# The loads between two layers, issued before the barrier instead of behind it

## The chip, the cores and the metric

The kernel runs on one core of one Trainium2 chip. The metric is the time of one execution on the device, in microseconds (us), as the median of several runs. The times of single instructions come from one profiled execution of the same kernel. TensorE is called PE, VectorE DVE, ScalarE ACT, GpSimd POOL and SyncE SP.

## The reference

Two layers follow each other over 3327 nodes with 256 features. Each is a graph attention over an adjacency matrix and then a mixture of experts, both added to the running x:

```python
x = x + _L0_gnn_ref(_layernorm(x), adj, L0_gnn_W, L0_gnn_r)
x = x + _L0_ffn_ref(_layernorm(x)[None], ...)[0]      # 8 experts, the best 2 of each node
x = x + _L1_gnn_ref(_layernorm(x), adj, ...)          # 4 heads, bias and a projection of the inputs
x = x + _L1_ffn_ref(_layernorm(x)[None], ...)[0]      # 8 experts, the best 2 of each node
```

What matters here is the seam between the second and the third line. The output of the first layer's experts is whole only when every expert's contribution has been added to every node; then a layer norm of it feeds the second layer's projections.

## The kernel before

The nodes are padded to 26 tiles of 128 rows. `X` in SBUF holds 26 x 256 float32 words per partition; `arena` holds everything else.

**The experts of layer 0** (`X0`) run over 59 tiles of slots. For each tile PE computes the hidden layer (L2308) and the output (L2347), DVE adds the bias and scales (L2427, L2430), and POOL scatters the 128 rows with an accumulating indirect DMA (L2296) into one of two totals in DRAM: `xd` for even tiles, `xe` for odd ones. Each scatter counts on one of two semaphores, `added[0]` and `added[1]`. While the experts run, `X` serves as room for their intermediates, so it can be loaded again only when the last scatters have read it. At the end of `tiles_gpsimd` POOL waits for both semaphores to be full.

**The program is cut into blocks.** In a block each engine has its own instruction list. At the end of a block every engine executes a drain and meets the others at a barrier (in the profile these instructions carry the line of the next block's `with`, L2502). Between the second block (layer 0) and the third (layer 1) there follow a clearing of the first layer's semaphores by POOL (L2558) and one more barrier (L2559).

**The third block begins with `A1.back_load`** (L484). It brings the two totals back: `xd` into `X` by four DMAs issued by SP, and `xe` into `A1.other` (a part of `arena`), its first piece by ACT and the other three by POOL. The pieces are cut at the pairs `PIECES = (0, 2, 5, 9, 13)` of tiles, so they hold 4, 6, 8 and 8 tiles of 128 KB. Each piece has a semaphore for each total. Behind its four loads SP runs `give_ones` (L2479): it adds one to each semaphore that has to start at one, those by which ACT, PE and DVE take turns over buffers among them. POOL adds up the two biases (L590), for which DVE waits before it begins with the pieces.

**The pieces** are then worked on as they come. DVE adds the two totals of a pair of tiles (L497, in `add_stats`), takes the statistics of both tiles (L501), and after the last pair of a piece computes mean and deviation (`norm_of`, L2452 to L2465 and L506; the square root, L2471, is ACT's). ACT normalizes a tile (L563), PE transposes it (L703), ACT copies it out (L548), and PE computes the projection (L713) and the attention's products (L716). DVE's `keep` (L514) adds the projection into `X` and frees its PSUM bank for PE. The order on each engine is written out by hand:

```python
for j in range(pieces[1]):          # pieces_vector, DVE
    add_stats(j)
norm_of(0)
for c in range(1, 4):
    for j in range(pieces[c], pieces[c + 1]):
        add_stats(j)
        if kept < pieces[c] - 2:
            for s in range(2):
                keep(kept, s)
            kept += 1
    norm_of(c)
```

So in the second piece (c = 1) no `keep` comes ahead of `norm_of(1)`. On ACT, `roots(1)`, the square root that `norm_of(1)` waits for, stands behind `turned(1, 1)`, the copy of the fourth transposed tile. The two banks of the projection are used in turn, so PE's projection of the third tile waits for the `keep` of the first.

Of the kernel before, what the change touches and what calls it, by code (L numbers as in the profile page):

```python
# [40 lines left out]
P = 128  # L41
NODES = 3327
T = 26
NP = T * P
D = 256
# [57 lines left out]
def program(nc, x_in, adjT, w0T, w0, r0, w1, w1T, uv1, proj_wT, bias1, proj_b1,  # L103
# [3 lines left out]
    with ctx:  # L107
# [142 lines left out]
        class SecondWeights:  # L250
# [4 lines left out]
            def __init__(self):  # L255
                self.w_cols = 4 * L1.HD + 2 * 4
                k = WORK_AT
                self.wmat = words(k, KC * self.w_cols)
                k += KC * self.w_cols
                self.proj = words(k, KC * D)  # L260
                k += KC * D
                self.attn_vec = words(k, KC * 8)
                k += KC * 8
                self.bias = words(k, D)
                k += D
                self.gate_in = words(k, KC * E)
                k += KC * E
                self.gate_bias = words(k, E)
                k += E
                assert k <= WORK_AT + self.ROOM  # L270
                self.end = k
                self.wT = words(WORK_AT - KC * D, KC * D)
                self.proj_b = words(WORK_AT - KC * D - D, D)
                self.center = edges[:, :]
                self.loaded = nc.alloc_semaphore(name="second_weights")
                self.center_ready = nc.alloc_semaphore(name="second_center_ready")
                self.vectors_ready = nc.alloc_semaphore(name="second_vectors_ready")
                self.vectors_copied = nc.alloc_semaphore(name="second_vectors_copied")

            def turned_sync(self, sp):  # L280
                sp.dma_start(self.wT.rearrange("p (k n) -> p k n", n=D),
# [53 lines left out]
        class Attention:  # L335
            def __init__(self, L, tag):
# [18 lines left out]
                k += 2 * D  # L355
                if H > 1:
                    self.conv = [words(k + s * NP // 2, NP // 2).bitcast(BF16) for s in range(2)]
                    self.other = words(k, T * D)
                    other_end = k + T * D
                    k += NP  # L360
                else:
                    self.center = words(k, P)
# [45 lines left out]
                self.w_loaded = second.loaded if H > 1 else sem(tag + "w_loaded")  # L408
                self.gate_loaded = sem(tag + "gate_loaded") if H == 1 else None
                self.center_ready = sem(tag + "center_ready") if H == 1 else None  # L410
                self.xd_back = [sem(f"{tag}xd_back{c}") for c in range(4 * (H > 1))]
                self.xe_back = [sem(f"{tag}xe_back{c}") for c in range(4 * (H > 1))]
                self.norm_known = sem(tag + "norm_known")
                self.far_known = sem(tag + "far_known")
                self.x_whole = sem(tag + "x_whole")
                self.stat = sem(tag + "stat")
                self.aggr = sem(tag + "aggr")
                self.var_ready = sem(tag + "var_ready")
# [6 lines left out]
                self.reach_best = sem(tag + "reach_best")  # L425
                self.reach_spread = sem(tag + "reach_spread")
                self.reach_ready = sem(tag + "reach_ready")
                self.far_steps = sem(tag + "far_steps")
                self.own_turned = sem(tag + "own_turned")
                self.own_copied = sem(tag + "own_copied")  # L430
                self.own_stored = sem(tag + "own_stored")
                self.pb = sem(tag + "pb")
                self.xn_ready = [sem(f"{tag}xn_ready{s}") for s in range(2)]
                self.tp_ready = [sem(f"{tag}tp_ready{s}") for s in range(2)]
# [17 lines left out]
                self.qt_ready = sem(tag + "qt_ready")  # L452
                self.qt_copied = sem(tag + "qt_copied")
                self.q_stored = sem(tag + "q_stored")
                self.conv_done = [sem(f"{tag}conv_done{s}") for s in range(2)]
                self.conv_used = [sem(f"{tag}conv_used{s}") for s in range(2)]
                self.rows_loaded = [sem(f"{tag}rows_loaded{s}") for s in range(2)]
                self.rows_free = [sem(f"{tag}rows_free{s}") for s in range(2)]
                self.prob_ready = [sem(f"{tag}prob_ready{s}") for s in range(self.slots)]
# [14 lines left out]
                                    + self.rows_free + self.exp_used + self.prob_used + self.banks_free + [self.acc_free])  # L474


            PIECES = (0, 2, 5, 9, PAIRS)

            def back_load(self, eng, which, first, last):

                to, of, landed = ((X, xd, self.xd_back), (self.other, xe, self.xe_back))[which]
                for c in range(first, last):
                    a, b = 2 * self.PIECES[c], 2 * self.PIECES[c + 1]
                    eng.dma_start(to[:, a * D:b * D].rearrange("p (t d) -> p t d", d=D),  # L484
                                  of[a * P:b * P, :].rearrange("(t p) d -> p t d", p=P)).then_inc(landed[c], 16)

            def pieces_vector(self, v, Q):

# [2013 lines left out]
        with nc.Block() as block:  # L2502
            @block.sync
            def _(sp):
                A0.gate_sync(sp, gate0, gate_b0)
                give_ones(sp, x0_ones)
                for t in (xs, xd, out):
                    sp.dma_start(t[NP:NP + P, 0:D], zeros[:, :].bitcast(F32)).then_inc(spare_clean, 16)
                sp.dma_start(xs[NP:NP + P, D:ROW], zeros[:, 0:8].bitcast(F32)).then_inc(spare_clean, 16)
                A0.single_sync(sp)  # L2510
                A0.gelu_sync(sp, X0.rows_stored)
                X0.route_sync(sp, None, m0b1, m0w2, xd, None)
                X0.tiles_sync(sp, m0w1, m0b1, m0b2, second)

            @block.gpsimd
            def _(pool):
                A0.center_gpsimd(pool)
                mask_loads_gpsimd(pool, A0.w_loaded)
                pool.dma_start(xe.rearrange("(t p) d -> p t d", p=P),
                               zeros[:, :].bitcast(F32).rearrange("p (o d) -> p o d", o=1).to_broadcast([P, T + 1, D])  # L2520
                               ).then_inc(xe_clean, 16)
                pool.wait_ge(xe_clean, 16)
                X0.route_gpsimd(pool, (A0.x_added, PAIRS))
                second.center_gpsimd(pool)
                pool.wait_ge(spare_clean, 64)
                X0.tiles_gpsimd(pool, [xd, xe], (A0.x_kept, 16 * PAIRS))

            @block.vector
            def _(v):
# [10 lines left out]
            @block.scalar  # L2540
            def _(a):
                A0.values_scalar(a)
                A0.first_rows_scalar(a)
                A0.single_scalar(a)
                X0.route_scalar(a, A0.last_gelu_scalar)
                X0.tiles_scalar(a)

            @block.tensor
            def _(pe):
# [18 lines left out]
        with nc.Block() as block:  # L2568
            @block.sync
            def _(sp):  # L2570
                A1.back_load(sp, 0, 0, 4)
                give_ones(sp, a1_ones + q1_ones + x1_ones)
                Q1.first_row_sync(sp)
                A1.own_row_sync(sp)
                sp.wait_ge(A1.far_known, 1)
                with sp.If(sp.value_load(is_far[0:1, 0:1], min_val=0, max_val=1) > 0):
                    A1.rows_sync(sp)
                    A1.attend_sync(sp)
                with sp.Else():
                    Q1.row_sync(sp)  # L2580
                X1.route_sync(sp, Q1.rows_final, m1b1, m1w2, out, (ln_g1, ln_b1))
                X1.tiles_sync(sp, m1w1, m1b1, m1b2)

            @block.gpsimd
            def _(pool):
                A1.back_load(pool, 1, 1, 4)
                A1.pieces_gpsimd(pool)
                X1.route_gpsimd(pool, (Q1.rows_final, 7))
                X1.tiles_gpsimd(pool, [out], (X1.x_spilled, 48))
# [17 lines left out]

            @block.scalar
            def _(a):
                A1.back_load(a, 1, 0, 1)  # L2610
                A1.pieces_scalar(a, Q1)
                Q1.early_scalar(a)
                a.wait_ge(A1.far_known, 1)
# [91 lines left out]
```

## Time and profile before

| | |
|---|---|
| median of 3 runs | 1764.57 us (1763.18 to 1766.04) |
| the profiled execution's own time | 1763.65 us |
| its span in the trace | 1761.9 us |
| PE busy | 1642.5 us, 93% |
| mean granted clock of PE | 0.98 of full speed |

All starts in the profile's rows are in us from the start of the span. A row of the order of time gives start, length, engine, line and operation, and in brackets how long the engine was idle before it and what ended that. SPq, ACTq and POOLq are the instruction queues of these engines; a DMA's row on them is the issue, not the transfer. The stretch between the layers lies at 705 to 735 us of the span.

### The profile page before, as it was taken

To read this page: it belongs to the slowest core of one execution; us is meant where nothing else is said; L and a number is where in the kernel's file an instruction comes from. 1 tells how busy PE (TensorE), PEld (TensorE's weight loads), DVE (VectorE), ACT (ScalarE), POOL (GpSimd) and SP (SyncE) were. 2 spreads that over 40 slices of the span, in tenths; PEclk is the share of its full clock that TensorE was granted. 3 is DMA by queue.
4 is the path that set the end of the run, shared out by engine and by line. 5 is a ranking of instruction groups with operands and counts; after the bars stand their busy time and mean duration, and the time that the engine had idled before them with its cause. 6 is when DMAs were issued, how large, how long until landed. Compare 5 with 4: busy or idle time off the path is not lost.

```text
span 1761.9 us, 41250 instructions
## 1 busy us (share of the span) xinstructions
PE 1642.5 (93%) x13276; PEld 1517.5 (86%) x13277; DVE 903.2 (51%) x2158; ACT 1019.0 (58%) x2334; POOL 356.7 (20%) x318
## 2 busy tenths in 40 slices
PE   4799999999799999489999999999989999999997
PEld 3678878888699999379999999999978999999997
DVE  4578868877512212468888878877750111111111
ACT  1143444445355555368989999899734555545443
POOL 2110000000166665320000000000012333333332
PEclk9889999999999999799999999999999999999999
DMA  9990000023478887400000000000366666666663
GB/s 161 107 171 21 1 19 9 9 89 127 123 191 213 225 211 179 161 8 20 13 16 19 9 19 13 15 20 12 130 249 216 185 183 183 179 179 179 179 180 94
DMA packets 93536, 190.33 MB, mean 108 GB/s; under 512 B 20777, under 2 KB 67625, under 8 KB 84617
## 3 DMA queue, kind: packets, MB, share of 16 engines
q1 hardware_dynamic: 60745, 139.50, 24.2%
q0 software_dynamic: 31360, 48.69, 17.5%
q10 hardware_dynamic: 1344, 1.05, 0.2%
q8 instruction: 46, 0.75, 0.2%
q14 instruction: 41, 0.34, 0.1%
HBM read 189.22 MB, written 33.22 MB: 126 GB/s over the span
## 4 chain that ended last, share of the span: by engine, by line
PE 52%; DVE 3%; DMA 2%; issue 1%; ACT 1%; POOL 0%; ACTq 0%; DVEq 0%; SPq 0%; POOLq 0%
PE bank L1783 24%; PE bank L2308 12%; PE bank L2347 11%; PE bank L713 1%; PE bank L716 1%; DMA X<-xd 1%; ACT arena L1485 1%; PE bank L2315 1%; DMA X<-m1b 0%; DVE arena L1621 0%; PE bank L2185 0%; DVE arena L1619 0%; PE bank L703 0%; DMA arena<-xs,slot_row 0%; PE bank L2192 0%
## 5 line engine op out<-in xcount | busy, mean ns | idle before, releaser
L1783 PE MATMUL bank<-arena 128*128 128x195 bf16 x5408 | 466.5, 247 | 13.5 <-DVE arena L1621 10.9
L1783 PEld LDWEIGHTS bank<-arena 128*128 128x128 fp8e4 x5408 | 463.2, 97 | 16.8 <-issue 15.8
L1485 ACT ACTIVATE arena<-arena,m_row 128x512 fp8e5<-128x512 f32 (+1 forms) x672 | 401.5, 678 | 43.8 <-DVE arena L1621 31.1
L2308 PEld LDWEIGHTS bank<-X,arena 128*128 128x128 f32 x2832 | 336.6, 194 | 9.9 <-issue 2.9
L2427 DVE TENSOR_TENSOR arena<-bank,X 128x256 f32<-128x256 f32 x118 | 50.1, 425 | 566.4 <-PE bank L2347 563.2
L2308 PE MATMUL bank<-X,arena 128*128 128x128 f32 x2832 | 339.5, 277 | 0.5 <-DMA arena<-m0w 0.4
L2347 PE MATMUL bank<-arena,X 128*128 x1416 | 325.0, 379 | 4.0 <-ACT X L2400 4.0
L1325 PE MATMUL bank<-arena 128*128 (+1 forms) x1352 | 313.3, 387 | 15.1 <-DVE arena L1231 15.0
L1325 PEld LDWEIGHTS bank<-arena 128*128 128x128 f32 x1352 | 253.3, 192 | 56.0 <-issue 20.9
L2347 PEld LDWEIGHTS bank<-arena,X 128*128 128x128 f32 x1416 | 259.9, 190 | 35.0 <-issue 4.4
L1183 ACT ACTIVATE bank<-arena,s_all 128x384 f32<-128x384 f32 (+1 forms) x234 | 133.7, 573 | 186.1 <-DVE arena L1223 184.3
L2400 ACT ACTIVATE X<-bank,arena 128x128 f32<-128x128 f32 x708 | 194.7, 378 | 20.9 <-issue 14.2
L1223 DVE SCALAR_TENSOR_TENSOR arena<-arena,d_all,bank 128x384 f32<-128x384 f32 (+1 forms) x234 | 139.0, 595 | 68.2 <-PE bank L1325 67.1
L2223 POOL IOTA arena<- 128x118 bf16 x2 | 1.6, 778 | 824.3 <-PE bank L2185 824.3
L2367 ACT ACTIVATE X<-bank,arena 128x128 f32<-128x128 f32 x118 | 47.6, 454 | 201.3 <-PE bank L2315 201.3
L2296 POOL DMA_INDIRECT out<-X,slot_row x59 | 93.4, 1583 | 270.9 <-DVE X L2430 267.8
L1619 DVE SCALAR_TENSOR_TENSOR arena<-arena 128x512 uint32<-128x512 uint32 (+1 forms) x168 | 109.6, 652 | 73.0 <-PE bank L1783 53.4
L2274 POOL DMA_INDIRECT arena<-xs,slot_row x118 | 116.6, 988 | 98.0 <-DVE slot_row L2132 59.6
L1231 DVE TENSOR_TENSOR arena<-arena 128x384 f32<-128x384 f32 (+1 forms) x234 | 125.0, 537 | 0.0
L1621 DVE SCALAR_TENSOR_TENSOR arena<-arena 128x512 uint32<-128x512 uint32 (+1 forms) x168 | 108.8, 648 | 0.0
L2363 ACT COPY X<-bank 128x256 f32<-128x256 f32 x59 | 22.0, 372 | 88.1 <-PE bank L2315 88.1
L2378 ACT ACTIVATE arena<-arena 128x256 f32<-128x256 f32 x118 | 69.7, 590 | 0.0
(250 smaller groups left out, 1359.6 us busy)
## 6 DMA issues: line engine op xcount, KB each, us to landing
arena<-m1w SPq DMA_DIRECT2D x67, 1024.0 KB, 13.3
arena<-m0w SPq DMA_DIRECT2D x67, 512.0 KB, 7.6
arena<-qd SPq DMA_DIRECT2D x25, 256.0 KB, 3.1
arena<-adjT POOLq DMA_DIRECT2D x13, 448.0 KB, 12.9
arena<-adjT POOLq DMA_DIRECT2D x13, 384.0 KB, 10.8
xs<-X SPq DMA_DIRECT2D x14, 256.0 KB, 2.6
xe<-zeros POOLq DMA_DIRECT2D x1, 3456.0 KB, 21.6
X<-x_in SPq DMA_DIRECT2D x2, 1664.0 KB, 11.8
```

What stands on the lines that cost most here:

```text
L1183: a.activation(self.exp_bank[s][:, 0:nt * P], self.rows[r][:, 0:nt * P], ACT.Exp, bias=s_all[:, at(c, 1)]).then_inc(self.exp_ready[s], 1)
L1223: v.scalar_tensor_tensor(out=self.prob[q][:, 0:w], in0=self.rows[r][:, W:W + w], scalar=d_all[:, at(c, 1)], in1=self.exp_bank[s][:, 0:w], ...
L1231: v.tensor_tensor(self.prob[q][:, 0:w], self.prob[q][:, 0:w], mask[:, at(c * NP + b * W, w)], ALU.min).then_inc(self.prob_ready[q], 1)
L1325: last = pe.matmul(bank[3 * r + n][:, 0:D + 1], self.prob[q][:, n * P:(n + 1) * P], V[:, at(c * VW, D + 1)], start=False, stop=False, skip ...
L1485: last = a.activation(self.sign[slot].bitcast(F8W)[:, q * W:q * W + nt * P], self.row[r][:, 0:nt * P], ACT.Sigmoid, scale=STEEP, bias=self ...
L1619: v.scalar_tensor_tensor(out=pos, in0=sg, scalar=1, in1=m, op0=ALU.logical_shift_left, op1=ALU.bitwise_and).then_inc(self.pos_ready, 1)
L1621: v.scalar_tensor_tensor(out=neg, in0=sg, scalar=0x08080808, in1=m, op0=ALU.bitwise_xor, op1=ALU.bitwise_and).then_inc(self.neg_ready[slot ...
L1783: last = pe.matmul(bank[rb * NT + n][:, kind * KW:(kind + 1) * KW], self.split[slot][kind].bitcast(F8)[:, q * W + n * P:q * W + (n + 1) * ...
L2274: pool.indirect_dma_start(self.rx[g % 4], None, xs[:, :], bass.IndirectOffsetOnAxis(ap=slot_row[:, g:g + 1], axis=0)).then_inc(self.rx_loa ...
L2308: last = pe.matmul(bank[2 * s + c // 4][:, c % 4 * P:(c % 4 + 1) * P], self.W1[s][:, k * HID + c * P:k * HID + (c + 1) * P], self.rxt[s][: ...
L2347: last = pe.matmul(bank[5 + s][:, 0:D], self.ht[s][:, c * P:(c + 1) * P], self.W2[:, at(e * (HC * D) + c * D, D)], start=(c == 0), stop=(c ...
L2400: last = a.activation(self.ht[s][:, c * P:(c + 1) * P], bank[2 * s + c // 4][:, c % 4 * P:(c % 4 + 1) * P], ACT.Gelu, bias=self.b1[:, at(e ...
```

## The change

The loads keep their sizes, pieces, destinations, queues and semaphores. What moves is the place where they are issued: at the end of the second block, on the same three engines, each behind a wait of its own for both `added` semaphores. The semaphores of the loads are now allocated with the second layer's weights, which are not cleared between the blocks, and `other` is the same room under another name. Some semaphores that only the second layer uses are no longer allocated for the first.

```diff
@@ class SecondWeights
+                self.other = words(k + 4 * D, T * D)
+                self.xd_back = [nc.alloc_semaphore(name=f"second_xd_back{c}") for c in range(4)]
+                self.xe_back = [nc.alloc_semaphore(name=f"second_xe_back{c}") for c in range(4)]
+
+            PIECES = (0, 2, 5, 9, PAIRS)
+
+            def back_load(self, eng, which, first, last, added):
+                to, of, landed = ((X, xd, self.xd_back), (self.other, xe, self.xe_back))[which]
+                for s in range(2):
+                    eng.wait_ge(added[s], 16 * (RUN_TILES // 2 + 1 - s))
+                for c in range(first, last):
+                    a, b = 2 * self.PIECES[c], 2 * self.PIECES[c + 1]
+                    eng.dma_start(to[:, a * D:b * D].rearrange("p (t d) -> p t d", d=D),
+                                  of[a * P:b * P, :].rearrange("(t p) d -> p t d", p=P)).then_inc(landed[c], 16)
@@ second block
                 X0.tiles_sync(sp, m0w1, m0b1, m0b2, second)
+                second.back_load(sp, 0, 0, 4, X0.added)
...
                 X0.tiles_gpsimd(pool, [xd, xe], (A0.x_kept, 16 * PAIRS))
+                second.back_load(pool, 1, 1, 4, X0.added)
...
                 X0.tiles_scalar(a)
+                second.back_load(a, 1, 0, 1, X0.added)
@@ third block
-                A1.back_load(sp, 0, 0, 4)
                 give_ones(sp, a1_ones + q1_ones + x1_ones)
...
-                A1.back_load(pool, 1, 1, 4)
                 A1.pieces_gpsimd(pool)
...
-                A1.back_load(a, 1, 0, 1)
                 A1.pieces_scalar(a, Q1)
```

## Rows read from the trace of the kernel before

**Rows 1.** The page: span, and busy time by engine
```profile
span 1761.9 us, 41250 instructions
PE 1642.5 (93%) x13276; PEld 1517.5 (86%) x13277; DVE 903.2 (51%) x2158; ACT 1019.0 (58%) x2334; POOL 356.7 (20%) x318
```

**Rows 2.** The order of time at the seam, 705 to 720 us
```profile
705.33 1.54 POOL L2296 DMA_INDIRECT xd<-X,slot_row  x1 [0.30 <-issue]
...
713.48 0.46 ACTq L484 DMA_DIRECT2D arena<-xe  x1
713.48 10.49 SPq L484 DMA_DIRECT2D X<-xd  x4
...
713.97 2.75 POOL L484 DMA_DIRECT2D arena<-xe  x3 [7.10 <-POOLq L2559]
...
716.71 0.76 POOL L590 TENSOR_TENSOR arena<-arena 128x256 f32<-128x256 f32 x1
717.63 0.14 DVE L517 MEMSET arena<- 128x104 f32 x1 [3.89 <-POOL arena L590]
719.41 0.69 DVE L497 TENSOR_TENSOR X<-X,arena 128x512 f32<-128x512 f32 x1 [1.64 <-DMA arena<-xe]
```

**Rows 3.** Instructions of the block's exit (L2502), durations in ns, starts in us
```profile
L2502 SPq DRAIN  x1: 7/7/7, 697.6 to 697.6; - x1
...
L2502 POOLq COMPARE_BRANCH  x1: 41/41/41, 709.1 to 709.1; - x1
L2502 POOLq DRAIN  x1: 2350/2350/2350, 709.3 to 709.3; - x1
L2502 SPq EVENT_SEMAPHORE  x1: 17/17/17, 711.8 to 711.8; - x1
```

**Rows 4.** Issues of the loads (L484) and SP's ones (L2479), 690 to 740 us
```profile
L484 SPq DMA_DIRECT2D X<-xd x4: 412/517/8899, 713.5 to 715.1; - x4
...
L2479 SPq EVENT_SEMAPHORE  x51: 17/17/17, 724.0 to 727.3; - x51
```

**Rows 5.** DMA issues, 700 to 780 us: KB each, median us to landing
```profile
arena<-xe POOLq DMA_DIRECT2D x2, 1024.0 KB, 12.4
...
X<-xd SPq DMA_DIRECT2D x1, 768.0 KB, 13.4
...
arena<-xe ACTq DMA_DIRECT2D x1, 512.0 KB, 5.8
```

**Rows 6.** The order of time in the first two pieces
```profile
724.13 1.09 ACT L563 ACTIVATE arena<-X,mv,rstd 128x256 f32<-128x256 f32 x2 [0.60 <-SPq L2479]
...
724.83 1.14 PE L703 MATMUL bank<-ident,arena 128*128 128x128 f32 x4 [18.83 <-ACT arena L563]
...
727.38 0.96 DVE L497 TENSOR_TENSOR X<-X,arena 128x512 f32<-128x512 f32 x1 [3.44 <-DMA X<-xd]
...
732.02 0.39 ACT L548 COPY arena<-bank 128x256 f32<-128x256 f32 x1
...
732.95 0.21 ACT L2471 ACTIVATE rstd<-rstd 128x6 f32<-128x6 f32 x1 [0.54 <-DVE rstd L2463]
...
733.50 0.75 DVE L514 TENSOR_TENSOR X<-bank,X 128x256 f32<-128x256 f32 x2
...
734.07 1.10 PE L713 MATMUL bank<-arena 128*128 128x256 f32 x4 [2.19 <-DVE X L514]
```

**Rows 7.** Stretches: us, busy (instructions) of PE, PEld, DVE, ACT, POOL; granted clock, DMA
```profile
709.00:710.00 1.00, 0.00 (x0) 0.00 (x0) 0.00 (x0) 0.00 (x0) 0.00 (x0) 0.50 0.00 0
...
730.00:731.00 1.00, 1.00 (x6) 0.89 (x5) 1.00 (x3) 0.44 (x3) 0.00 (x0) 1.00 1.10 348
```

**Rows 8.** The order of time at the first block's end, 0 to 10 us
```profile
0.81 1.46 SPq L182 DMA_DIRECT2D X<-x_in  x2
...
3.73 5.59 SPq L609 DMA_DIRECT2D slot_w<-gate  x1
3.74 0.21 POOL L614 MEMSET arena<- 128x128 f32 x1 [0.31 <-POOLq L2481]
```

More of the change, by code:

```diff
@@ L357, in __init__ @@
                     self.conv = [words(k + s * NP // 2, NP // 2).bitcast(BF16) for s in range(2)]
-                    self.other = words(k, T * D)
+                    self.other = second.other
                     other_end = k + T * D
@@ L410, in __init__ @@
                 self.center_ready = sem(tag + "center_ready") if H == 1 else None
[L411 to L415, printed above, removed]
+                self.xd_back, self.xe_back = second.xd_back, second.xe_back
+                self.norm_known = sem(tag + "norm_known") if H > 1 else None
+                self.far_known = sem(tag + "far_known") if H > 1 else None
+                self.x_whole = sem(tag + "x_whole") if H > 1 else None
                 self.stat = sem(tag + "stat")
@@ L427, in __init__ @@
                 self.reach_ready = sem(tag + "reach_ready")
[L428 to L431, printed above, removed]
+                self.far_steps = sem(tag + "far_steps") if H > 1 else None
+                self.own_turned = sem(tag + "own_turned") if H > 1 else None
+                self.own_copied = sem(tag + "own_copied") if H > 1 else None
+                self.own_stored = sem(tag + "own_stored") if H > 1 else None
                 self.pb = sem(tag + "pb")
@@ L454, in __init__ @@
                 self.q_stored = sem(tag + "q_stored")
-                self.conv_done = [sem(f"{tag}conv_done{s}") for s in range(2)]
-                self.conv_used = [sem(f"{tag}conv_used{s}") for s in range(2)]
+                self.conv_done = [sem(f"{tag}conv_done{s}") for s in range(2 * (H > 1))]
+                self.conv_used = [sem(f"{tag}conv_used{s}") for s in range(2 * (H > 1))]
                 self.rows_loaded = [sem(f"{tag}rows_loaded{s}") for s in range(2)]
@@ L474, in __init__ @@
                                     + self.rows_free + self.exp_used + self.prob_used + self.banks_free + [self.acc_free])
[L477 to L485, printed above, removed]
+            PIECES = SecondWeights.PIECES
             def pieces_vector(self, v, Q):
```

## The prediction

> **What bounds the kernel now.** I read the page first. PE is busy 93% of the span [rows 1], so what a seam costs is the time that PE stands still in it. Then the order of time at the seam. The last scatter is issued at 705.33 and the loads start at 713.48; DVE touches the first pair of tiles at 719.41 [rows 2], and PE starts at 724.83 after 18.83 us of idleness [rows 6]. The exit's instructions split the gap: POOL leaves its waits for the last scatters at about 709.07 (its branch stands at 709.1), then drains for 2.35 us from 709.3 and so is the last at the barrier, at 711.65 [rows 3]. SP's first issue at 713.48 is 1.83 us behind that: two barriers and a clearing of semaphores.
>
> So the loads could start 713.48 - 709.15 = 4.33 us earlier (0.08 from the waits' end to the issue, my choice). That is 0.25% of the span and the most that the change can bring, if PE's start moved as far. The question is what holds the barrier then.
>
> **SP's issues.** The issue rows show it. SP has four loads of X; three of them take about half a us each, but the longest issue takes 8.90 us, and the four together occupy SP for 10.49 us, 713.48 to 723.97 [rows 2, 4]. This is time of SP itself, not of a transfer in the background: its next instructions, the 51 ones, begin at 724.0 [rows 4], and ACT's first normalization waited 0.60 us for one of them [rows 6]. Today nothing else of weight stands behind these issues. After the change the block's exit does.
>
> The kernel has one more place with loads outstanding at a barrier. In the first block SP issues two loads in 1.46 us and passes the barrier at once; its next DMA, in the second block, then takes 5.59 us to issue [rows 8]. So outstanding loads don't hold a barrier, but an issue that SP cannot get rid of holds SP. Here the held issue is the fourth of four and lies ahead of the barrier.
>
> **The sum, part by part.**
>
> 1. *Removed:* the loads from the third block. POOL gets to its addition of the biases (L590) without 2.75 us of issues [rows 2], and the ones no longer stand behind SP's issues. ACT's table load and DVE's memset start as before.
>
> 2. *Added:* on SP, ACT and POOL two waits each on semaphores that POOL waits for already; the wait on POOL costs nothing, being met. Nothing is queued behind the waits on SP and ACT but the drain, and they were idle there: SP's drain stands at 697.6 [rows 3].
>
> 3. *Moved on SP:* four issues from 709.15. With the same transfers on the same queues against the same neighbours I take the same 10.49 us: done at 719.64. The lower bound is four issues of 0.5 us (2.1 us), should nothing be held; that is a rival below.
>
> 4. *Moved on POOL:* three issues, starting about 0.5 us behind SP's as now (713.97 against 713.48), 709.6 to 712.4, then the drain. Its 2.35 us behind a scatter that has landed [rows 3] give 714.75. The trace doesn't show a POOL drain behind loads in flight. Its lower bound is nothing, its upper one the landing of the last piece of xe, at about 729 (713.97 + 2 issues of 0.9 + 12.4 and a little more, the second of the two 1024 KB loads being later than their median [rows 2, 5]) less 4.35: 724.9. I take 2.35, since L590 ran on POOL at 716.71, right behind the three issues and long before their landing [rows 2, 5]. Then POOL is hidden behind SP.
>
> 5. *Moved on ACT:* one issue of 0.46 us, hidden behind SP.
>
> 6. *The barrier:* SP is the last, at 719.7. With the 1.83 us of today the third block starts at 721.5, against 713.48.
>
> 7. *The first piece:* it has landed long before (ACT's load of xe takes 5.8 us [rows 5], 715.0). What DVE waits for instead is POOL's bias addition: at once (the first block has POOL at work 0.01 us behind SP's first instruction [rows 8]), 0.76 us long, then 0.16 to DVE's memset, 0.14 for that, and some 0.07 to L497 [durations in rows 2]. So L497 starts 1.17 us into the block, at 722.7, against 719.41: 3.3 us later. The wait of ACT for SP's ones goes, worth some 0.16 us. ACT's normalization, and PE's start, are 3.1 us later.
>
> 8. *The second piece:* DVE came to it at 727.38, after waiting 3.44 us for X [rows 6]. That load lands 13.4 us behind an issue at about 713.95 [rows 5], 727.35; after the change at 723.0, so this wait is gone. DVE gets there by its own work, 722.7 + 4.5 = 727.2. Its chain is 0.2 us earlier than now: the 3.44 us of waiting absorb DVE's later start.
>
> 9. *Where PE picks up:* PE's third projection starts at 734.07, released by keep (L514) at 733.50, which stands behind the square root of the second piece at 732.95 [rows 6]. That root waited 0.54 us for DVE; on ACT it stands behind the fourth tile's copy, 732.02 to 732.41 [rows 6], which follows PE and so is 3.1 us later, at 735.5. The root becomes bound by ACT and PE, not by DVE: 3.1 - 0.5 = 2.6 us later than now. PE's clock is no part of it: the granted clock is 0.50 (1.2 GHz) from 709 on, after PE had stopped, and 1.00 (2.4 GHz) in the stretch from 730 [rows 7], 5 us behind PE's start; later starts shift this, they don't add to it. From 734 on PE, ACT and DVE go in step and no load is awaited, so the 2.6 us stay.
>
> **Sum:** +2.6 us. On the profiled execution's span of 1761.9 that is 1764.5, on its own time of 1763.65 it is 1766.3. That time lies 0.9 us below the median of the runs, to which I add: **1767.2 us**, +0.15%. About 0.2% (3.5 us) is what a measurement of this kernel can tell from no change.
>
> The Trainium skill (DMA: Bandwidth & Descriptors, "Issuing engines are not separate DMA queues") says that starting a DMA costs its sequencer a time usually small beside the DMA. By that rule SP would be at the barrier by 711.3, and the result would be the first rival's. The 8.90 us issue speaks against it here; three of the four issues agree with it.
>
> **Rivals.**
>
> *SP is not held ahead of the barrier.* For it: three short issues, and the two loads of the first block [rows 4, 8]. Against it: the same four loads with the same neighbours held SP. POOL's drain then decides, 714.75, and the block starts at 716.6; L497 at 717.75, 1.7 us earlier. PE's start comes 1.8 us earlier and by step 9 the root's ACT side 2.3 us, DVE's side 4.3 us (the second piece's landing at 723.0). The later one counts: -2.3 us, 1762.3. Only if POOL's drain vanished too (block at 714.3, L497 at 715.5) would it be the full -4.3 us, 1760.2; from a third block ahead of about 715 on it is faster by over 0.2%.
>
> *POOL's drain waits for its own loads.* For it: no drain in the trace stands behind loads in flight, and the one behind the scatters is the longest thing on the exit. Against it: POOL computed L590 with them in flight [rows 2]. It decides from 719.7 on. With the last landing, 724.9, the block starts at 726.8 and L497 at 728.0; PE's start is 8.4 us later, PE's third projection 7.9: 1772.5. If it ends halfway, with the second piece of POOL's, about 721.9, it is +4.9: 1769.4.
>
> The Trainium skill (DMA: Bandwidth & Descriptors, "SWDGE vs HWDGE vs iDMA") has GpSimd's cores write the descriptors of POOL's DMAs; a drain that waits for this writing would be a milder form of this rival. No row here shows when it ends.
>
> *SP is held for another length.* Its fourth issue ends as transfers progress. While POOL's xe flows, SP's loads crawl: X's 768 KB took 13.4 us, 1024 KB of xe 12.4 us with later issues [rows 5]. Each 0.5 us by which POOL's loads start sooner or later behind SP's moves the end by about as much; I allow -1.5 to +1.6 us, so +1.1 to +4.2 in all.
>
> **How the numbers follow.** Forecast with its own spread 0.62 (a fifth of it above +3.5 us); SP not held 0.12 (a third of it with a short drain); POOL's drain longer than SP 0.18; something at the block's edge that no step names 0.08, mostly within 0.2%. Faster 0.04 + 0.02, about 0.06. Slower 0.12 + 0.17 + 0.02, 0.31. Within 0.2%: 0.63. The range goes from the first rival's 1762.3 to between the drain's two values, with a run-to-run spread of 1.4 us in mind: 1762.3 to 1771.5. The likeliest case alone: 1765.7 to 1768.8.
>
> **What the profile would show.** Right: SP's four issues begin near 709.15 and last some 10.5 us; SP's exit drain stands at 719.6 and POOL's has ended long before; the block starts at 721.5; L497 waits for POOL's L590 and not for a DMA; no DMA wait at the second piece; PE idle 22 us, from 706 to 728; the root of the second piece follows ACT's copy at once. Wrong: an issue of 1 us at most on SP and a start near 716.6 (first rival), or a POOL drain of over 7 us (second). Should PE's third projection start near 734 although the block starts at 721.5, step 9 is wrong and the median stays.

## The result, and the profile after

The changed kernel takes 1772.1 us (median of 6 runs, 1770.64 to 1774.72), the kernel before 1764.45 us beside it. The ratio is 1.0045 with a 95% interval of 1.0035 to 1.0056: slower by 7.9 us, and the interval is clear of 1. The forecast was 1767.2 us with a range to 1771.5. The time lies outside it, at the price that the second rival had (1772.5). The profiled execution took 1772.3 us, its span is 1770.6 us.

The order of time at the seam, after, beside [rows 2] and [rows 6] (every line of `kernel.py` is moved by 6 or more, so L497 is now L503, L590 is L596, L563 is L569, L713 is L719, and the loads' L484 is L292):

```profile
704.02 1.54 POOL L2302 DMA_INDIRECT xd<-X,slot_row  x1 [0.30 <-issue]
...
707.85 0.41 ACTq L292 DMA_DIRECT2D arena<-xe  x1
707.98 8.23 SPq L292 DMA_DIRECT2D X<-xd  x4
708.50 2.75 POOL L292 DMA_DIRECT2D arena<-xe  x3 [2.94 <-DMA xd<-X,slot_row]
726.28 1.28 ACT L2477 ACT_TABLE_LOAD   x1 [25.89 <-PEq L2568]
726.32 0.72 POOL L596 TENSOR_TENSOR arena<-arena 128x256 f32<-128x256 f32 x1 [15.07 <-POOLq L2568]
...
727.19 0.67 DVE L503 TENSOR_TENSOR X<-X,arena 128x512 f32<-128x512 f32 x1 [0.65 <-issue]
...
732.43 1.14 PE L709 MATMUL bank<-ident,arena 128*128 128x128 f32 x4 [27.73 <-ACT arena L569]
...
741.71 1.10 PE L719 MATMUL bank<-arena 128*128 128x256 f32 x4 [1.55 <-DVE X L520]
```

The loads do start early, 3.83 us behind the start of the last scatter instead of 8.15. Then all engines stand still from 711 to 726 us. The exit's instructions, beside [rows 3], tell whom they stand for:

```profile
L2508 POOLq DRAIN  x1: 14848/14848/14848, 709.3 to 709.3; - x1
L2508 SPq DRAIN  x1: 124/124/124, 716.3 to 716.3; - x1
L2508 SPq EVENT_SEMAPHORE  x1: 17/17/17, 724.4 to 724.4; - x1
```

(The three numbers are the shortest, median and longest duration in ns, then come the first and last start.) SP comes to its drain at 716.3, held by its fourth issue as forecast, if for less long. But POOL's drain now takes 14.85 us instead of 2.35 and ends at 724.2; the barrier opens with it. The row of POOL's drain begins at 709.3, before POOL's third issue (710.33): it begins when the instruction queue comes to it and not when the engine is free, so it is the drain's end that counts. The DMA issues of the changed kernel, 710.6 to 711 us, with KB each and us to landing, have the last load of POOL, issued at 710.33 (6.31 us behind the scatter):

```profile
arena<-xe POOLq DMA_DIRECT2D x1, 1024.0 KB, 13.2
```

It lands at 723.5, 0.7 us ahead of the drain's end. PE's third projection comes 37.69 us behind the start of the last scatter (741.71 - 704.02), before it was 28.74 (734.07 - 705.33 in [rows 2, 6]): 8.95 us lost at the seam. In this one profiled execution the third block from there on to the last scatter took 0.9 us more than in that of before; among all kernels here the same stretch varies from 1020.8 to 1023.9 us, so that can't be called an effect of the change.

### The profile page after: what moved, and what is told of

Read it like the earlier page. It is cut to its first block, busy times and chain, and to the rows that moved or that the text cites. A ratio compares the mean times of both kernels' runs of the same rounds, so it can differ in the third digit from the quotient of the medians.

```text
span 1770.6 us, 41249 instructions
## 1 busy us (share of the span) xinstructions
PE 1640.7 (93%) x13276; PEld 1517.2 (86%) x13277; DVE 902.4 (51%) x2158; ACT 1018.9 (58%) x2334; POOL 356.6 (20%) x318
## 3 DMA queue, kind: packets, MB, share of 16 engines
q10 hardware_dynamic: 1344, 1.05, 0.2%
## 4 chain that ended last, share of the span: by engine, by line
PE 52%; DVE 3%; issue 1%; ACT 1%; DMA 1%; POOL 0%; ACTq 0%; DVEq 0%; POOLq 0%
PE bank L1789 24%; PE bank L2314 11%; PE bank L2353 11%; PE bank L719 1%; PE bank L722 1%; ACT arena L1491 1%; PE bank L2321 1%; DMA X<-m1b 0%; DVE arena L1627 0%; PE bank L2191 0%; PE bank L709 0%; DVE arena L1625 0%; DMA arena<-xs,slot_row 0%; PE bank L2198 0%; PE bank L2181 0%
```

## The experiments

The table counts every time from the start of the last scatter into `xd` or `xe` in that execution, since the scatter itself moves by some us from run to run. "Block" is the first instruction of the third block, "first sum" DVE's first addition of the totals, "third" PE's third projection, released by the first `keep`. The last column is the ratio of times to the kernel before, measured on the same chip.

| kernel | POOL's drain | block | first sum | third | ratio (95%) |
|---|---|---|---|---|---|
| before | 2.35 | 8.15 | 14.08 | 28.74 | 1 |
| changed | 14.85 | 22.26 | 23.17 | 37.69 | 1.0045 (1.0035 to 1.0056) |
| pool_waits | 2.60 | 24.28 | 25.19 | 38.68 | 1.0067 (1.0051 to 1.0084) |
| pool_behind | 2.35 | 10.41 | 14.56 | 29.19 | 1.0003 (0.9992 to 1.0015) |
| pool_early | 10.82 | 18.25 | 23.92 | 37.67 | 1.0060 (1.0040 to 1.0079) |
| no_pool | 2.35 | 8.05 | 9.27 | 22.45 | 0.9974 (0.9963 to 0.9985) |
| no_pool_again | 2.35 | 8.06 | 9.32 | 23.56 | 0.9966 (0.9952 to 0.9979) |
| no_pool_third | 2.35 | 7.83 | 9.11 | 22.20 | 0.9987 (0.9978 to 0.9997) |
| all_hw | 2.35 | 12.07 | 12.98 | 26.15 | 0.9998 (0.9989 to 1.0007) |
| pool_one | 9.46 | 15.61 | 16.83 | 30.25 | 1.0014 (1.0005 to 1.0023) |
| warm | 2.35 | 9.26 | 10.17 | 22.05 | 0.9968 (0.9958 to 0.9978) |
| before_sp_waits | 4.70 | 6.10 | 11.78 | 26.02 | 0.9977 (0.9967 to 0.9986) |
| no_pool_sp_waits | 4.75 | 7.44 | 9.20 | 22.69 | 0.9963 (0.9950 to 0.9977) |
| warm_short | 4.71 | 7.47 | 9.20 | 21.38 | 0.9965 (0.9952 to 0.9977) |

All columns but the last come from one profiled execution of each kernel, the last one from 4 to 12 executions. The two can differ: no_pool_third has its third projection 6.5 us earlier than before and gains 2.3 us by the ratio, all_hw 2.6 and 0.4, while pool_early loses 8.9 and 10.6. The rest of the kernel varies by about as much (1020.8 to 1023.9 us, above). So the columns tell where at the seam the time goes, and the ratio what the kernel gains or loses.

### What does POOL's drain wait for?

**pool_waits** adds to the changed kernel waits for the landings of POOL's own loads:

```diff
                 second.back_load(pool, 1, 1, 4, X0.added)
+                for c in range(1, 4):
+                    pool.wait_ge(second.xe_back[c], 16)
```

> The changed kernel, with one thing added: at the end of the second block POOL waits for the semaphores of its own three loads of xe before it comes to the block's exit. Theory (POOL's drain, 14.85 us in the changed kernel, lasts until its own loads have landed, about 0.6 us behind the landing): the wait takes the place of the drain, the block's end stays within 0.5 us unless a fixed 2.35 us follows each drain behind a DMA, then it is up to 2 us later; time 1772 to 1774. Rival (the drain lasts for another reason, such as POOL writing out its descriptors or SP's queue): the drain keeps much of its length behind the wait, 5 us or more, and the time rises by as much, 1777 or more.

The exit's instructions in its profile:

```profile
L2508 SPq DRAIN  x1: 123/123/123, 718.2 to 718.2; - x1
L2508 POOLq DRAIN  x1: 2595/2595/2595, 725.6 to 725.6; - x1
```

With the landings awaited, the drain is short again: what filled it was the time to the landing. But 2.6 us remain behind the landing, where the changed kernel has 0.7, and the block starts 2.0 us later than there, as expected. So at a block's end at which POOL has issued DMAs its drain takes 2.35 us or more from its own start, and lasts until the landing where that is later. The first block, in which POOL issues none, shows that this floor isn't there for every drain. Its exit's drain in the kernel before:

```profile
L2481 POOLq DRAIN  x1: 1016/1016/1016, 2.5 to 2.5; - x1
```

It ends at 3.49, 0.07 us behind POOL's last instruction, and POOL's drains at the seam's further steps take 0.05 to 0.26 us. The third projection is 1.0 us later than in the changed kernel and not 2.0, since PE's clock came back sooner there (see below). The time of 1775.6 us lies above the 1772 to 1774 expected; the kernel before was at 1765.3 beside it, and the interval of the ratio overlaps the changed kernel's.

**pool_early** leaves only POOL's loads ahead of the barrier:

```diff
-                second.back_load(sp, 0, 0, 4, X0.added)
-                second.back_load(a, 1, 0, 1, X0.added)
                 second.back_load(pool, 1, 1, 4, X0.added)
@@ third block
+                second.back_load(sp, 0, 0, 4)
+                second.back_load(a, 1, 0, 1)
```

> Only POOL's three loads go ahead of the barrier; SP's four and ACT's one are issued behind it, as in the kernel before. Theory (the drain waits for POOL's own loads): alone on the DMA engines they land about 12 us behind their issue, the drain lasts some 11 to 12 us, the third block starts 9 to 10 us later than in the kernel before, its first piece comes 5.4 us behind that; PE's third projection is 8 to 10 us later: 1772.5 to 1775. Rival (the drain is long only because SP's queue is full): drain 2.35 to 4 us, block 3 us later, 1766 to 1768.

Its drain at the exit:

```profile
L2508 POOLq DRAIN  x1: 10821/10821/10821, 714.6 to 714.6; - x1
```

And its DMA issues from 715.7 to 716.3 us, with KB and us to landing:

```profile
arena<-xe POOLq DMA_DIRECT2D x1, 1024.0 KB, 9.2
```

The same three loads, without the traffic of SP and ACT beside them, land after 9.2 us instead of 13.2, and the drain falls by as much, from 14.85 to 10.82. The last landing is at 724.7 (issued at 715.57), the drain ends at 725.4. The third projection is 8.9 us later than before, within the 8 to 10 expected; the time of 1776.1 us is 1 us above its range. A drain that waited only until POOL has written its descriptors would have no reason to follow the traffic of other queues, unless that writing were itself held by it; the traces don't show the writing.

**pool_one** builds on no_pool (below) and gives POOL a single load, the second piece of xe:

```diff
-                second.back_load(a, 1, 0, 3, X0.added)
+                second.back_load(a, 1, 0, 1, X0.added)
+                second.back_load(a, 1, 2, 3, X0.added)
+                second.back_load(pool, 1, 1, 2, X0.added)
```

> As no_pool, but the second piece of xe (768 KB), issued by ACT there, is issued by POOL, ahead of the barrier. Theory (the drain lasts until POOL's own load has landed): this load is smaller and the first of its queue, so it lands some 8 to 9 us behind its issue and the drain takes 8 to 9 us; the block starts some 5.5 to 6.5 us later than in no_pool, and PE's third projection about as much: 1765.5 to 1767.5. Rival (a drain behind a DMA issue is long whatever the load, or its length goes by the number of loads): a drain near 14.85 us or near 2.35 us, and 1772 or 1760.

Its drain at the exit, and the issue among the DMA issues from 700 to 780 us:

```profile
L2508 POOLq DRAIN  x1: 9458/9458/9458, 710.3 to 710.3; - x1
```

```profile
arena<-xe POOLq DMA_DIRECT2D x1, 768.0 KB, 8.9
```

The drain takes 9.46 us, from 710.29 to 719.75; the load, issued at 710.31, landed at 719.2. The block starts 7.6 us later than in no_pool, 1 to 2 us more than I expected, because the barrier and the drain's tail came on top of the 9.4; the ratio, 1.0014, is 0.3 to 0.5% above no_pool's. So the length of the drain goes with the landing of what POOL itself has outstanding: 9.46, 10.82 and 14.85 us in three kernels, each ending 0.6 to 0.7 us behind the landing.

**before_sp_waits** is the kernel before with POOL's two last waits moved to SP, at the end of the second and of the third block. The same waits, on another engine:

```diff
@@ tiles_gpsimd, at its end
+            def all_added(self, eng):
                 for s in range(2):
-                    pool.wait_ge(self.added[s], 16 * (RUN_TILES // 2 + 1 - s))
+                    eng.wait_ge(self.added[s], 16 * (RUN_TILES // 2 + 1 - s))
@@ second and third block, SP
                 X0.tiles_sync(sp, m0w1, m0b1, m0b2, second)
+                X0.all_added(sp)
...
                 X1.tiles_sync(sp, m1w1, m1b1, m1b2)
+                X1.all_added(sp)
```

> The kernel before, with the waits for the last scatters moved from POOL to SP, at the end of the second and of the third block: POOL comes to its drain right behind its last issue. Theory (POOL's drain itself lasts until its DMAs have landed, and the 2.35 us behind a landed scatter are a floor that starts with the drain): each drain starts some 2.3 us earlier and ends within 1 us of the scatter's landing, so each of the two exits is 1.5 to 2 us earlier: 1761 to 1762 beside 1764.5, and everything between the two exits is earlier by 1.5 to 2 us. Rival (the 2.35 us come behind the last landing whatever the start, as in the kernel where POOL waited first): no change.

The drains of POOL and SP at the seam in its profile:

```profile
L2504 POOLq DRAIN  x1: 4700/4700/4700, 703.8 to 703.8; - x1
...
L2504 SPq DRAIN  x1: 7/7/7, 708.3 to 708.3; - x1
```

And at the kernel's end:

```profile
L2571 POOLq DRAIN  x1: 4565/4565/4565, 1751.8 to 1751.8; - x1
...
L2571 SPq DRAIN  x1: 7/7/7, 1756.1 to 1756.1; - x1
```

Without its wait POOL's drain begins at 703.8, 0.4 us ahead of the last scatter's row, takes 4.70 us and is done at 708.5, 4.3 us behind the scatter's start instead of 6.3. The last count of that scatter arrives at 707.95 in this trace, so the drain ends 0.5 us behind the landing once more. The block starts 2.05 us earlier, and the end of the kernel comes 4.57 us behind the last scatter instead of 6.43, 1.9 us earlier. The ratio of 0.9977 is 4.1 us, about the sum of the two. So the drain lasts until accumulating scatters have landed too, and at both of these exits of the kernel before its 2.35 us had been paid behind a wait that already covered the landing.

### What is left when POOL is out of the way?

**pool_behind** leaves the loads of SP and ACT ahead of the barrier and puts only POOL's three behind it:

```diff
                 second.back_load(sp, 0, 0, 4, X0.added)
                 second.back_load(a, 1, 0, 1, X0.added)
-                second.back_load(pool, 1, 1, 4, X0.added)
@@ third block
+                second.back_load(pool, 1, 1, 4)
```

> SP's four loads and ACT's one stay ahead of the barrier; POOL's three go back behind it. Theory (POOL's drain alone holds the barrier): the drain falls to 2.35 us; SP's fourth issue, no longer beside xe's traffic, ends some 6 us behind its first, so the third block starts 3.3 us later than in the kernel before; POOL's bias addition comes behind its 2.75 us of issues; PE's start 1.5 us later than in the kernel before, its third projection 1 to 2 us later: 1764.5 to 1767, 5 to 8 us below the changed kernel. Rival (loads in flight of any queue hold the exit): the block's end stays at the landing of SP's loads or POOL's drain stays over 8 us, and the time stays at 1770 or more.

The issues on SP in its profile (durations in ns as min/median/max, then the first and the last start):

```profile
L292 SPq DMA_DIRECT2D X<-xd x4: 407/524/2998, 709.6 to 711.2; - x4
```

And the exit's drains in it:

```profile
L2508 POOLq DRAIN  x1: 2350/2350/2350, 709.7 to 709.7; - x1
...
L2508 SPq DRAIN  x1: 123/123/123, 714.3 to 714.3; - x1
```

The whole loss of the change is gone: 1.0003. This kernel has all the other parts of the change too, the moved semaphores among them, so they cost nothing that can be measured. Now SP is last at the barrier, 2.3 us behind POOL, and the block starts 2.26 us late, where I expected 3.3, since SP's four issues took 4.59 us and not 6. SP and ACT drain in 0.12 and 0.15 us with their loads in flight: their drains don't wait for landings. The third projection stands 0.45 us later than before, less than the 1 to 2 expected.

**no_pool** takes POOL's loads away altogether. SP and ACT issue three pieces each ahead of the barrier and the fourth behind it:

```diff
-                second.back_load(sp, 0, 0, 4, X0.added)
+                second.back_load(sp, 0, 0, 3, X0.added)
-                second.back_load(a, 1, 0, 1, X0.added)
+                second.back_load(a, 1, 0, 3, X0.added)
-                second.back_load(pool, 1, 1, 4, X0.added)
@@ third block
+                second.back_load(sp, 0, 3, 4)
                 give_ones(sp, a1_ones + q1_ones + x1_ones)
...
+                second.back_load(a, 1, 3, 4)
                 A1.pieces_scalar(a, Q1)
```

> No load on POOL. Ahead of the barrier SP issues the first three pieces of xd and ACT the first three of xe; the fourth of each follows on the same queue at the start of the third block. Theory (the early start is worth something as soon as neither POOL's drain nor a held issue stands at the exit): drain 2.35 us, block start as in the kernel before; the first pair is added about 4.5 us earlier than before, the wait for the second piece is gone, PE's third projection is 4 to 5.5 us earlier: 1759 to 1761, 0.2 to 0.3% below the kernel before. Rival (loads in flight hold the exit whatever the queue, or ACT's third issue is held as SP's fourth was): the block starts 3 us or more later and the time is 1764 or more.

The order of time at its seam:

```profile
705.14 1.54 POOL L2302 DMA_INDIRECT xd<-X,slot_row  x1 [0.30 <-issue]
708.90 5.61 ACTq L292 DMA_DIRECT2D arena<-xe  x4
709.02 6.38 SPq L292 DMA_DIRECT2D X<-xd  x4
713.22 0.72 POOL L596 TENSOR_TENSOR arena<-arena 128x256 f32<-128x256 f32 x1 [6.54 <-POOLq L2567]
...
714.41 0.69 DVE L503 TENSOR_TENSOR X<-X,arena 128x512 f32<-128x512 f32 x1 [0.16 <-DMA X<-xd]
```

The two rows of issues run from the first issue to the end of the fourth, which stands behind the barrier; the time at the barrier is in them. The issues by themselves:

```profile
L292 ACTq DMA_DIRECT2D arena<-xe x4: 431/548/1314, 708.9 to 713.2; - x4
L292 SPq DMA_DIRECT2D X<-xd x4: 407/545/2202, 709.0 to 713.2; - x4
```

The fourth, issued 3.2 us behind the third, is held for 2.20 us on SP and 1.31 us on ACT.

The block starts where it did before, but the first piece is there: DVE adds it 4.8 us earlier than before (9.27 against 14.08), and PE's third projection is 5.2 to 6.5 us earlier in the three executions profiled, where I expected 4 to 5.5. The kernel was timed in two more sets:

> The same kernel as no_pool, timed in more rounds and beside its variants: 0.25 to 0.3% below the kernel before, 1759 to 1761.

> no_pool once more, as the measure for its variants on this chip: 0.25 to 0.35% below the kernel before.

The three ratios are 0.9974, 0.9966 and 0.9987; the last one's interval overlaps the other two only at its lower end. The gain is some 2 to 6 us. The first two sets are as expected, if the second by a little more than the 0.3%; the last one, 0.13% where I expected 0.25 to 0.35%, is below, and I have no cause for the spread.

**all_hw** puts the fourth pieces of no_pool ahead of the barrier too:

```diff
-                second.back_load(sp, 0, 0, 3, X0.added)
+                second.back_load(sp, 0, 0, 4, X0.added)
-                second.back_load(a, 1, 0, 3, X0.added)
+                second.back_load(a, 1, 0, 4, X0.added)
@@ third block
-                second.back_load(sp, 0, 3, 4)
-                second.back_load(a, 1, 3, 4)
```

> As no_pool, but the fourth pieces are issued ahead of the barrier too, on the same queues: SP and ACT issue all four each, POOL none. In no_pool the four issues took SP 6.4 us and ACT 5.6 us. Theory (an issue that its queue doesn't take at once holds the barrier when it lies ahead of it, as the prediction had it, only shorter than it said): SP and ACT reach the exit some 6.4 us behind their first issue, 3.7 us later than POOL does in no_pool; the third block, the first pair's addition and PE's third projection are 3.5 to 4.2 us later than in no_pool: 1763.5 to 1765. POOL's drain stays 2.35 us. Rival (the held issue costs nothing there): as no_pool, 1760.

The issues in its profile, columns as above:

```profile
L292 ACTq DMA_DIRECT2D arena<-xe x4: 432/548/3684, 707.5 to 709.1; - x4
L292 SPq DMA_DIRECT2D X<-xd x4: 408/546/4517, 707.6 to 709.2; - x4
```

And its drains at the exit:

```profile
L2508 POOLq DRAIN  x1: 2350/2350/2350, 707.6 to 707.6; - x1
L2508 ACTq DRAIN  x1: 153/153/153, 712.8 to 712.8; - x1
L2508 SPq DRAIN  x1: 124/124/124, 713.8 to 713.8; - x1
```

This is the mechanism of the forecast by itself. The fourth issue is held, 4.52 us on SP and 3.68 us on ACT; with it ahead of the barrier the block starts 4.0 us later than in no_pool and the third projection 2.6 to 4.0 us later. The gain of no_pool (0.9966 beside it on the same chip) is used up: 0.9998, although the third projection of the profiled execution is still 2.6 us earlier than before. The place of the fourth load alone decides between the two. My expectation took the 6.4 and 5.6 us of no_pool's rows for time in issues; the barrier is in them, as said above, and that SP's four issues took 6.15 us here agrees with them by chance. The time of 1762.1 us is below the 1763.5 to 1765 expected; the kernel before was at 1762.8 beside it.

### PE's clock

**warm** is no_pool with products into a spare bank that nobody reads:

```diff
                 second.vectors_tensor(pe)
+                for _ in range(30):
+                    pe.matmul(bank[7][:, 0:P], ident[:, :], ident[:, :], start=True, stop=True)
@@ third block
+                for _ in range(24):
+                    pe.matmul(bank[7][:, 0:P], ident[:, :], ident[:, :], start=True, stop=True)
                 A1.values_tensor(pe)
```

> As no_pool, with products that nobody reads (identity by identity into a spare bank): 30 at the end of PE's second block and 24 at the start of its third, where PE stood idle. Theory (PE's first tiles run at the granted clock of 0.5 because PE had stopped, and PE's path, not DVE's, now sets the third projection): the clock is back at 1.0, or never falls, when the first tile comes; the root of the second piece comes when DVE has its input, 1.8 to 2 us earlier than in no_pool: 1757.5 to 1759. Rival (prediction's step 9: the clock is no part of it): no change against no_pool; should the 24 products run at half clock and end behind ACT's first normalized tile, up to 1 us slower.

Stretches of the changed kernel (columns as in [rows 7]), where PE's first transposition is at 732.43:

```profile
737.00:738.00 1.00, 1.00 (x4) 0.77 (x3) 0.28 (x2) 0.58 (x3) 0.00 (x0) 0.50 0.00 0
738.00:739.00 1.00, 1.00 (x5) 0.83 (x4) 0.00 (x0) 0.22 (x1) 0.00 (x0) 0.77 0.00 0
739.00:740.00 1.00, 1.00 (x7) 0.75 (x5) 0.00 (x0) 0.01 (x1) 0.00 (x0) 1.00 0.00 0
```

And of warm, where it is at 718.98:

```profile
710.00:712.00 2.00, 1.04 (x10) 0.85 (x8) 0.00 (x0) 0.00 (x0) 0.00 (x0) 1.00 1.06 371
712.00:714.00 2.00, 1.14 (x10) 1.17 (x11) 0.43 (x3) 0.70 (x1) 0.73 (x1) 1.00 1.07 375
718.00:720.00 2.00, 1.44 (x10) 0.81 (x9) 1.93 (x6) 1.56 (x4) 0.92 (x2) 1.00 1.09 379
```

In warm the granted clock stays at 1.00 (2.4 GHz) all through. From the first sum to the third projection it takes 11.88 us; the changed kernel takes 14.52, no_pool 13.1 to 14.2. So the half clock (1.2 GHz) costs 1.2 to 2.6 us on this stretch in these kernels, where PE and ACT, not DVE, set the third projection.

The other traces bear this out. In the ten executions profiled in which ACT and PE set that root at a clock that had fallen (changed, pool_waits, pool_behind, pool_early, the three of no_pool, all_hw, pool_one and no_pool_sp_waits), the clock came back 3.1 to 6.3 us behind PE's first transposition, and the third projection followed that transposition by 7.83 to 9.39 us: about half a us more for each us that the clock stayed at 0.50. In warm it is 6.63. The clock's return moves by itself: in three executions of no_pool it came after 3.1, 3.3 and 5.4 us.

The kernel as a whole isn't measurably faster than no_pool (0.9968). The 30 products were too many: PE came to the barrier after POOL and the block starts 1.2 us later. That leaves little of the gain beside two of no_pool's executions (22.05 against 22.45 and 22.20); beside the third, on the same chip, the third projection is 1.5 us earlier, which the timing doesn't show.

**warm_short** takes no_pool_sp_waits (below), with 12 products ahead of the barrier and 24 behind it.

> no_pool_sp_waits with products that nobody reads, 12 at the end of PE's second block (not 30, whose drain came to the barrier 1.2 us after POOL's) and 24 at the start of its third. Theory (PE at half clock sets the third projection in no_pool): if the clock is back when the first tile comes, the second piece's root comes with DVE's input, 1.5 to 3 us earlier than in no_pool_sp_waits. Rival: the clock falls in the 4 us between the two groups, the 24 products take 11 us instead of 5.6, and PE's start is later by 3 to 5 us.

Stretches of it:

```profile
714.00:717.00 3.00, 0.00 (x0) 0.00 (x0) 0.00 (x0) 0.00 (x0) 0.00 (x0) 1.00 0.53 148
717.60:719.00 1.40, 1.31 (x7) 1.34 (x8) 0.31 (x2) 0.00 (x0) 0.73 (x1) 0.66 1.05 367
719.00:721.00 2.00, 2.00 (x11) 2.00 (x11) 1.58 (x4) 1.28 (x1) 0.00 (x0) 0.50 1.08 385
722.00:724.00 2.00, 2.00 (x21) 2.00 (x20) 1.46 (x10) 0.27 (x2) 0.00 (x0) 1.00 1.09 384
```

It came out between the two theories. PE stood still from 713.62 to 717.69. The granted clock was still 1.00 in that gap; it fell at 718.05, with the second group of products under way, and was back at 721.46, ahead of PE's first tile at 724.75. The 24 products took 7.2 us and ended as that tile came. The third projection is 1.3 us earlier than in no_pool_sp_waits (21.38 against 22.69); the timing can't tell the two apart (0.9965 and 0.9963).

### The best version

**no_pool_sp_waits** is no_pool with both of POOL's last waits gone. At the second block's end SP and ACT wait for the same semaphores anyway, at the third's SP does, by `X1.all_added(sp)` as above.

> no_pool with POOL's waits for the last scatters given up at the end of the second block (SP and ACT wait there for the same semaphores) and moved to SP at the end of the third. Theory: at the kernel's end 1.5 to 2 us earlier, as in the kernel before; at the seam next to nothing, 0 to 0.5 us, since there the first pair of tiles already waited 0.16 to 0.19 us for its own load: 1.5 to 2.5 us below no_pool. Rival (the drain's floor follows the landing): as no_pool.

The end of the kernel comes 1.8 to 2.1 us earlier than in no_pool, the seam gives nothing: DVE's first sum is at 9.20 us, bound by the landing of its load. At 0.9963 (0.9950 to 0.9977), 6.5 us below the kernel before and about 0.8% below the changed one, this has the lowest ratio; warm_short, warm and no_pool_again (0.9965 to 0.9968) can't be told from it. Beside no_pool on the same chip it is 4 us faster where I expected 1.5 to 2.5; the traces account for some 2 us of it, at the kernel's end.

## Why the prediction was wrong

*Step 4 failed.* It said that POOL's drain would take 2.35 us, "since L590 ran on POOL at 716.71, right behind the three issues and long before their landing". That row shows only that a computing instruction of POOL doesn't wait for POOL's DMAs. A drain does. The runs show it four times: the drain ends 0.6 to 0.7 us behind the landing of POOL's last DMA in the changed kernel, pool_early and pool_one, and is back at 2.6 us when the landings are awaited before it; and pool_behind, where nothing but POOL's loads goes back behind the barrier, has the loss gone. Whether the drain waits for the landing itself, or for descriptors whose writing is held up by the traffic until about then, no trace tells; for the kernel it is the same time. The bound was worked out, 724.9 for the drain's end; measured from the same scatter, it ended 20.2 us behind it, against 19.6. So was the price: 7.9 us at the third projection, measured 8.95 at the seam and 7.9 in the ratio. That the time came within 0.4 us of 1772.5 is in part chance, since the seam lost 1.05 us more than priced. The chance given to it, 0.18, was too low, and the range ended at 1771.5, below the price of this very rival. The trace had no row of a drain behind loads in flight on POOL, and I let the nearest favourable row decide.

*Step 3 had the mechanism right and its size wrong.* An issue that its queue doesn't take holds the engine and, ahead of a barrier, everybody: all_hw shows it alone, 4.0 us. But 10.49 us for SP's four issues was 8.23 in the changed kernel, 4.59 in pool_behind and 4.69 in pool_early, where POOL's loads aren't beside them, and 6.15 in all_hw, where ACT's are. The held issue alone took 8.90 before, then 6.64, 3.00, 2.84 and 4.52 us. How long it lasts goes with the other queues' traffic; why the changed kernel's is 2.3 us shorter than that of before, with the same neighbours, stays open. Behind POOL's drain it cost nothing.

*Steps 1, 2 and 5* held: the issues begin 3.83 and 3.96 us behind the scatter (forecast 3.82), ACT's issue and the waits cost nothing. Of *step 6* the way from the last drain to the block held, 2.1 us, 0.3 more than taken; but the last drain is POOL's and not SP's, by step 4.

*Steps 7 and 8* held in kind. DVE waits for no DMA at either piece; from the block's start to the first sum it takes 0.91 us, where I had 1.17.

*Step 9* found the right chain: in the changed kernel the root of the second piece follows ACT's copy of the fourth tile. It was wrong that the clock is no part of it. In the kernel before the granted clock returned 4.6 us behind PE's start and DVE set the third projection, so the half clock was covered; in the changed kernel it returned 6.0 us behind PE's start with nothing to cover it. From PE's start to the third projection it is 9.28 us there, 9.24 before, where step 9 said that 0.5 us would be won back. Where the clock returns earlier, that much and more is won back: 8.24 us in pool_waits, with the return at 3.9 us. So the 0.5 us between the seam's loss and what step 9 makes of a start 8.9 us later is the late return in this one execution. Why the return varies, no run shows.

The rule of the Trainium skill (DMA: Bandwidth & Descriptors, "Issuing engines are not separate DMA queues"), that starting a DMA costs its engine little, held here for three loads of each row of four (0.4 to 0.8 us each), and not for the fourth (2.84 us or more on SP).

## What to carry to other kernels

Before DMAs are moved ahead of a barrier, ask of each issuing engine what it does between its last issue and the barrier: here a drain of POOL's lasted until its own loads had landed, while SP's and ACT's didn't, so a prefetch across a barrier belongs on SP or ACT, and only as many issues as the queue takes without holding the engine. A wait on POOL for its own last DMAs right ahead of such a drain is paid on top of the drain; another engine can hold it for nothing. And where the trace before has no row for a wait that a change creates, its upper bound deserves more than a tail of the chances.

## What the runs showed of the hardware

- POOL's drain at a block's end ended 0.5 to 0.7 us behind the landing of POOL's own last DMA, for loads (drains of 9.46, 10.82 and 14.85 us) as for accumulating scatters (4.5 to 4.75 us). With the DMAs already landed it took 2.34 to 2.60 us, and 1.02 us in the first block, where POOL had issued none. SP's and ACT's took 0.12 to 0.15 us with loads in flight.
- The fourth issue in a row of loads of 512 to 1024 KB held SP for 2.84 to 8.90 us and ACT for 3.68 us. The first three took 0.4 to 0.8 us each. Issued 3.2 us behind the third, the fourth took 2.20 us on SP and 1.31 us on ACT (no_pool); 10.7 us behind it, 0.38 us (SP in pool_one).
- After PE had stood still, its granted clock came back from 0.50 to 1.00 between 3.1 and 6.3 us behind its first tile (4.6 us in the kernel before, 6.0 in the changed one), by different times in executions of one kernel. It stayed at 1.00 in warm, where PE stood still for 1.8 us between the two groups of products, and fell in warm_short, where it did for 4.1 us, 0.4 us after PE had begun again.
